# Both attentions of a fused two-layer kernel in new orders, the first one's sums of values in two halves

## The chip, the cores and the metric

One core of one Trainium2 chip. The metric is the device time of one execution in microseconds (us). TensorE is called PE, VectorE DVE, ScalarE ACT, GpSimd POOL and SyncE SP, as in the profile.

## What is computed

Two transformer layers over x of shape [8, 512, 128], all float32, each an attention and a feed-forward part with a layer norm behind each:

```
x = layernorm(x + attention0(x))      # 16 heads of 8, relative positions clipped to +-64
x = layernorm(x + ffn0(x))
x = layernorm(x + attention1(x))      # 16 heads of 8, sinusoidal relative shift
x = layernorm(x + ffn1(x))

# attention0, per batch and head (8 x 16 = 128 heads):
scores = Q K^T + take(Q pos_key^T, clip(k - q + 64)) + take(K pos_query^T, clip(q - k + 64))^T
probs  = softmax(scores * scale);  ctx = probs V
```

Attention1 differs in the form of its position scores; softmax and the sum of values are the same.

## The kernel before, in words

The program has five stages: an opening (projections, `opening`), the first attention (`attention(0)`, in the code `rel` is true), a mixing stage (feed-forward 0 and the projections of layer 1), the second attention (`attention(1)`) and a dense stage. An attention goes over 128 heads of 512 queries and 512 keys. One **step** works for one head `j`; the engines run it in parallel from five programs whose orders are written out by hand and joined by semaphores: `tensor_step`, `vector_step`, `scalar_step` and `sync_step`. Eight steps are unrolled in a loop; four of them (`GROUP`) make a group.

What a step does, with its four tiles k = 0 to 3 of 128 queries (`NT` = 4):

- `score_tile` (L821, L823, in the first attention also L827) makes a score tile in one of four PSUM banks, `score_ahead` tiles ahead (6 in the first attention, 7 in the second). It waits for the exp that empties its bank. In the first attention L827 writes a corner into the shared bank `other`, and so waits for the mask copy of the tile before.
- DVE: `mix` (L908, first attention only) copies that corner in by a mask; `finish` (L920) adds a band of position scores; `row_max` (L928) takes the maximum. `key_out` (L755, first) and `edge_out` (L933, second) copy a product of the position part out of PSUM, once in a step.
- ACT: `exp_tile` (L980), 4 or 5 tiles ahead; `copy_turned` (L987) copies a turned block out of PSUM; `corr_out` (L761, first attention); `group_out` (L993) copies the sums of a finished group, on the last step of each group, behind the second turned block.
- PE: `turn` (L842) transposes the 512 x 128 probabilities of key block k, four transposes of 128 x 128, into bank 5 or 6. `weigh` (L855) is the sum of values: for key block k of four heads of the group before, four matmuls of 32 columns by 512 queries (two instructions each), all adding to `cbank`. One such k is done in each step, so a group is summed during the four steps after it. `key_side` (L741) and `correction` (L748, L749) in the first attention, `edge` (L722) in the second, make the position part for a head some steps ahead. Bank 5 is shared with `key_side`, bank 6 with `correction`; in the second attention bank 4 takes `edge`.
- SP issues every DMA. In the first attention in each step: `shear_b_write` (L646), `shear_b_read` (L652), `head_load` (two halves, L608 and L609), `shear_a_read` (L640), `shear_a_write` (L634 for the next head); on a group's last step also `tab_load` (L621), three `offset_load` (L628, L629), the group's store (L671) and the next values (L673). `shear_b_write` waits for `corr_out`. The head loaded in one step is `key_side`'s in the next (`LOAD_AHEAD` 8, `KEY_AHEAD` 7).

The order of PE in a step before the change, and of ACT:

```
PE,  first:   score turn0 SUM | score turn1 key_side | score turn2 | score turn3 | correction
PE,  second:  score turn0 SUM | score turn1 edge     | score turn2 | score turn3
ACT, both:    exp copy0 | exp copy1 [group_out] | exp copy2 | exp copy3 | (first: corr_out)
DVE, first:   4 x (mix, row_max, finish), key_out behind the second
DVE, second:  4 x (finish, row_max), edge_out
```

The waits of `turn`: in the first attention turn0 for the last copy of the head before, turn1 for `corr_out`, turn2 for copy1, turn3 for `key_out`; in the second each turn for the copy two before.

Of the kernel before, what the change touches and what calls it, by code (L numbers as in the profile page):

```python
# [21 lines left out]
B, T, C = 8, 512, 128  # L22
H = 16
DH = C // H
NT = T // 128
NHEAD = B * H
# [31 lines left out]
VW = 32  # L58
BASE = 32
# [5 lines left out]
def build(nc, t):  # L65

    top = ExitStack()
    with top:
# [430 lines left out]
        def attention(layer):  # L499

            rel = layer == 0
# [287 lines left out]
            def program(block, before, after):  # L789
# [72 lines left out]
                def tensor_step(pe, i, j, left, weighed=True):  # L862
                    own = Head(i, j)
                    for k in range(NT):
                        if left >= (k + score_ahead) // NT:
                            score_tile(pe, *ahead(i, j, k, score_ahead))
                        turn(pe, own, k)
                        if k == 0 and weighed:
                            weigh(pe, Head(i, j - j % GROUP - GROUP), j % GROUP)
                        if not rel and k == 1 and left >= CORR_AHEAD:  # L870
                            pe.wait_ge(corr_copied, BASE + own.n + CORR_AHEAD)
                            edge(pe, Head(i, j + CORR_AHEAD), corr_bank)
                        if rel and k == 1 and left >= KEY_AHEAD:
                            pe.wait_ge(copied, BASE + 4 * own.n + 1)
                            key_side(pe, Head(i, j + KEY_AHEAD), key_bank)
                    if rel and left >= CORR_AHEAD:
                        pe.wait_ge(copied, BASE + 4 * own.n + 3)
                        correction(pe, Head(i, j + CORR_AHEAD))

                @block.tensor  # L880
                def _(pe):
# [16 lines left out]
                    for k in range(NT):  # L898
                        weigh(pe, Head(loops, FIRST + last - GROUP), k)
# [34 lines left out]

                @block.vector
                def _(v):
# [11 lines left out]
                    def vector_step(i, j, left):  # L948
                        for k in range(NT):

                            if left >= (k + score_ahead) // NT:
                                if rel:
                                    mix(v, *ahead(i, j, k, score_ahead))
                                else:
                                    finish(v, *ahead(i, j, k, score_ahead))
                            if left >= (k + score_ahead - 1) // NT:
                                row_max(v, *ahead(i, j, k, score_ahead - 1))
                            if rel and left >= (k + score_ahead) // NT:
                                finish(v, *ahead(i, j, k, score_ahead))
                            if not rel and k == 3 and left >= CORR_AHEAD:  # L960
                                edge_out(v, Head(i, j + CORR_AHEAD))
                            if rel and k == 1 and left >= KEY_AHEAD:
                                key_out(v, Head(i, j + KEY_AHEAD), key_bank)

                    for j in range(FIRST):
                        vector_step(0, j, NHEAD)
# [3 lines left out]
                    for j in range(last):  # L970
                        vector_step(loops, FIRST + j, last - 1 - j)
                        after.vector_tail(v, last - 1 - j)

# [22 lines left out]
                def _(act):  # L996
# [3 lines left out]
                    def scalar_step(i, j, left, weighed=True):  # L1000
                        own = Head(i, j)
                        for k in range(NT):
                            if left >= (k + exp_ahead) // NT:
                                exp_tile(act, *ahead(i, j, k, exp_ahead))
                            copy_turned(act, own, k)
                            if k == 1 and weighed and j % GROUP == GROUP - 1:
                                group_out(act, Head(i, j - j % GROUP - GROUP))
                        if rel and left >= CORR_AHEAD:
                            corr_out(act, Head(i, j + CORR_AHEAD))

# [8 lines left out]
                    group_out(act, Head(loops, FIRST + last - GROUP))  # L1019
# [1015 lines left out]
```

## Time and profile before

| | us |
|---|---|
| median of 3 runs | 1965.22 (1956.04 to 1966.07) |
| profiled execution | 1965.38 |
| its span on the core | 1963.2 |
| first attention, undisturbed part | 200 to 830 of the span |
| second attention, undisturbed part | 1065 to 1580 of the span |

Busy shares over the whole span: PE 88%, DVE 74%, ACT 75%, POOL 4%; DMA queues 67% of the 16 engines. The shares are means over five stages with different limits, so they are to be read by stretch. In a timeline row the columns are the start, the duration, the engine, the line of kernel.py, the operation, its tiles and shapes, the number of instructions merged into the row, and in brackets the idle time of that engine ahead of it and what ended it. PEld is the weight load of PE, SPq a DMA issue of SP.

### The profile page before, as it was taken

The numbers are of one execution on the slowest core, as the hardware profiler recorded it, in microseconds if no ns is written. First come the engines' busy times: TensorE is split into PE (matmuls) and PEld (weight loads), VectorE is DVE, ScalarE is ACT, GpSimd is POOL, SyncE is SP. The second block draws the span as 40 slices with busy tenths as digits, with TensorE's granted clock in tenths as the row PEclk, the third lists the DMA queues.
The fourth block names the chain that finished last, engine by engine and source line by source line (L and its number), as shares of the span: only waits on it lengthen the run. The fifth ranks groups of instructions, "written<-read, shape, count | busy, mean of one in ns | idle before, by whom it ended". The sixth has DMA issues, their size and how long they took to land.

```text
span 1963.2 us, 44049 instructions
## 1 busy us (share of the span) xinstructions
PE 1728.0 (88%) x11694; PEld 1040.9 (53%) x11694; DVE 1446.4 (74%) x3501; ACT 1475.8 (75%) x2605; POOL 80.2 (4%) x102
## 2 busy tenths in 40 slices
PE   5479999999999999977767999999999989999998
PEld 2145555555555555545444655655666544545454
DVE  5568888888888888876977888888888873244322
ACT  4458888888888888876878999999999974232221
POOL 0000000000000000003520000000000000000000
PEclk8679999999999999998978999999999989999999
DMA  6788888888888888865999777777777771001000
GB/s 207 281 249 256 268 265 261 263 263 266 264 266 265 264 259 264 259 183 158 342 338 297 217 213 210 213 212 214 210 214 213 209 211 44 21 27 37 21 6 11
DMA packets 414359, 404.44 MB, mean 206 GB/s; under 512 B 36969, under 2 KB 334561, under 8 KB 414177
## 3 DMA queue, kind: packets, MB, share of 16 engines
q1 hardware_dynamic: 414305, 403.80, 67.3%
q8 instruction: 24, 0.39, 0.1%
q14 instruction: 30, 0.25, 0.0%
HBM read 226.89 MB, written 176.30 MB: 205 GB/s over the span
## 4 chain that ended last, share of the span: by engine, by line
PE 48%; issue 13%; ACT 11%; DVE 9%; SPq 8%; DMA 6%; POOL 0%; DVEq 0%; ACTq 0%; POOLq 0%
PE bank L842 12%; PE bank L1847 11%; PE bank L855 9%; ACT a_probt L987 5%; PE bank L821 4%; DVE a_negmax L928 3%; DMA a_stks<-stack 3%; ACT a_prob L980 3%; DVE a_keyside L755 2%; DVE bank L908 2%; PE bank L823 2%; PE bank L1839 1%; PE bank L1840 1%; PE bank L1868 1%; PE bank L722 1%
## 5 line engine op out<-in xcount | busy, mean ns | idle before, releaser
L980 ACT ACTIVATE a_prob<-bank,a_negmax 128x512 f32<-128x512 f32 x1024 | 738.2, 721 | 44.7 <-DVE a_negmax L928 43.2
L928 DVE TENSOR_REDUCE a_negmax<-bank 128x1 f32<-128x512 f32 x1024 | 698.3, 682 | 0.2 <-issue 0.2
L842 PE MATMUL bank<-ident,a_prob 128*128 128x128 f32 x4096 | 646.5, 281 | 56.8 <-ACT a_probt L987 49.0
L987 ACT COPY a_probt<-bank 128x512 f32<-128x512 f32 x1024 | 619.5, 605 | 97.4 <-PE bank L842 85.6
L842 PEld LDWEIGHTS bank<-ident,a_prob 128*128 128x128 f32 x4096 | 451.5, 142 | 174.9 <-issue 70.7
L920 DVE TENSOR_TENSOR bank<-bank,a_band 128x128 f32<-128x128 f32 (+3 forms) x1024 | 349.5, 341 | 81.6 <-PE bank L823 66.5
L821 PE MATMUL bank<-a_stks 74*128 74x192 bf16 (+7 forms) x1024 | 324.9, 317 | 31.5 <-ACT a_prob L980 29.4
L855 PE MATMUL bank<-a_probt,a_vs 128*32 128x512 f32 x2048 | 275.3, 612 | 12.8 <-ACT a_probt L987 12.8
L821 PEld LDWEIGHTS bank<-a_stks 74*128 74x128 bf16 (+1 forms) x1024 | 100.2, 98 | 260.0 <-ACT a_prob L980 215.0
L908 DVE COPY_PREDICATED bank<-a_mask,bank 128x128 f32<-128x128 uint32 (+1 forms) x512 | 139.4, 272 | 112.0 <-PE bank L827 109.7
L823 PE MATMUL bank<-a_stks 74*128 74x320 bf16 (+5 forms) x768 | 201.8, 263 | 0.0
L1913 DVE TENSOR_TENSOR d_drop<-bank,d_s 128x128 f32<-128x128 f32 x32 | 7.1, 283 | 170.4 <-PE bank L1868 170.4
L748 PE MATMUL bank<-ident,a_sheared 128*128 128x128 f32 x512 | 106.5, 285 | 19.4 <-DMA a_sheared<-shear_a 15.0
L827 PE MATMUL bank<-a_stks 74*128 74x128 bf16 (+1 forms) x512 | 110.4, 216 | 10.9 <-DVE bank L908 2.7
L1847 PE MATMUL bank<-d_ha,d_h1T 128*128 128x512 f32 x256 | 112.3, 592 | 0.0
L1847 PE MATMUL bank<-d_hb,d_h2T 128*128 128x512 f32 x256 | 111.2, 592 | 0.0
L755 DVE COPY a_keyside<-bank 128x512 f32<-128x512 f32 x128 | 87.2, 681 | 24.8 <-PE bank L741 24.4
L749 PE MATMUL bank<-a_tabs,a_stks 65*128 65x128 bf16 x512 | 97.5, 225 | 0.0
L761 ACT COPY a_corr<-bank 128x512 f32<-128x512 f32 x128 | 76.4, 597 | 23.2 <-DMA shear_b<-a_corr 11.9
L748 PEld LDWEIGHTS bank<-ident,a_sheared 128*128 128x128 f32 x512 | 74.3, 145 | 34.7 <-issue 21.5
L1898 ACT ACTIVATE d_hb<-bank,d_fs 128x512 f32<-128x512 f32 x32 | 22.0, 687 | 90.6 <-PE bank L1847 90.6
L1903 ACT ACTIVATE d_hc<-bank,d_fs 128x512 f32<-128x512 f32 x32 | 22.0, 687 | 87.6 <-PE bank L1847 87.6
(178 smaller groups left out, 1622.7 us busy)
## 6 DMA issues: line engine op xcount, KB each, us to landing
a_band<-shear_b SPq DMA_DIRECT2D x128, 512.0 KB, 4.9
shear_a<-a_keyside SPq DMA_DIRECT2D x128, 256.0 KB, 3.7
a_sheared<-shear_a SPq DMA_DIRECT2D x128, 256.0 KB, 3.7
shear_b<-a_corr SPq DMA_DIRECT2D x128, 256.0 KB, 2.8
shear_e<-a_corr SPq DMA_DIRECT2D x128, 256.0 KB, 2.2
a_band<-shear_e SPq DMA_DIRECT2D x128, 256.0 KB, 3.1
a_stks<-stack SPq DMA_DIRECT2D x256, 96.0 KB, 3.0
a_stks<-stack SPq DMA_DIRECT2D x384, 48.0 KB, 2.5
```

The source lines that it names most:

```text
L748: pe.matmul(corr_bank[:, q], sheared[h.slot % 4][:, q], ident[:, :], is_transpose=True, start=True, stop=False)
L755: v.tensor_copy(keyside[h.slot % 4][:, :], source[:, :]).then_inc(key_copied, 1)
L821: last = pe.matmul(score[:, 0:c], k[:, qlo, q], k[:, keys, 0:c], start=True, stop=True)
L823: last = pe.matmul(score[:, c:T], k[:, qhi, q], k[:, keys, c:T], start=True, stop=True)
L842: last = pe.transpose(turned_bank[k][:, n * 128:(n + 1) * 128], prob[h.slot % 2][:, n, k * 128:(k + 1) * 128], ident[:, :])
L855: pe.matmul(cbank[32 * j:32 * j + VW, :], vs[g][:, at:at + VW], probt[h.slot + j][:, k, :], start=(k == 0), stop=(k == NT - 1)).then_inc(p ...
L908: v.copy_predicated(score[:, a:e], mask[:, 0:e - a], other[:, 0:e - a]).then_inc(fixed, 1)
L920: v.tensor_tensor(score[:, a:e], score[:, a:e], band[h.slot % bands][:, n, w:w + e - a], ALU.add).then_inc(added, 1)
L928: v.tensor_reduce(negmax[h.slot % 2][:, n:n + 1], score[:, :], AX.X, ALU.max, negate=True).then_inc(maxed, 1)
L980: nc.scalar.activation(prob[h.slot % 2][:, n, :], score[:, :], ACT.Exp, bias=negmax[h.slot % 2][:, n:n + 1]).then_inc(exped, 1)
L987: nc.scalar.copy(probt[h.slot][:, k, :], turned_bank[k][:, :]).then_inc(copied, 1)
L1847: last = pe.matmul(dst[:, :], w[:, k, 128 * m:128 * m + 128], src[:, k, :], start=(k == 0), stop=(k == KH - 1))
```

## The change

The four step functions are split into one for each attention, written out without the loop over k. In the first attention `weigh` takes a range of columns: in the steps of a group's second to fourth head it does queries 0 to 255 behind turn1 and queries 256 to 511 behind turn2; in the step of the group's first head it does all 512 behind turn1. In the second attention turn0 and turn1 stand together, then a score tile, then the sum of all 512; turn2 and turn3 stand together; `edge` moves to the end of the step. ACT's order becomes exp, copy, copy, exp, exp, copy, (group copy in the first), and so on. The group copy of the second attention moves from ACT to DVE, behind the second maximum of the last step of a group. SP's program is not touched.

```
PE,  first:   score turn0 score turn1 SUM(a) key_side score turn2 SUM(b) score turn3 correction
PE,  second:  score turn0 turn1 score SUM score turn2 turn3 score edge
ACT, first:   exp copy0 copy1 exp exp copy2 [group_out] exp copy3 corr_out
ACT, second:  exp copy0 copy1 exp exp copy2 copy3 exp
DVE, second:  finish max finish max [group copy] finish max finish max edge_out
```

```diff
-                def weigh(pe, h, k):
+                def weigh(pe, h, k, cols):
...
-                        pe.matmul(cbank[32 * j:32 * j + VW, :], vs[g][:, at:at + VW], probt[h.slot + j][:, k, :],
-                                  start=(k == 0), stop=(k == NT - 1)).then_inc(pv_mm, 1)
+                        part = pe.matmul(cbank[32 * j:32 * j + VW, cols], vs[g][:, at:at + VW], probt[h.slot + j][:, k, cols],
+                                         start=(k == 0), stop=(k == NT - 1 and cols.stop == T))
+                        if cols.stop == T:
+                            part.then_inc(pv_mm, 1)
...
+                def shifted_tensor_step(pe, i, j, left, weighed=True):
                     own = Head(i, j)
...
+                    score_ahead_of(pe, i, j, left, 0)
+                    turn(pe, own, 0)
+                    score_ahead_of(pe, i, j, left, 1)
+                    turn(pe, own, 1)
+                    if weighed:
+                        weigh(pe, Head(i, j - j % GROUP - GROUP), j % GROUP, slice(0, T // 2 if j % GROUP else T))
+                    if left >= KEY_AHEAD:
+                        pe.wait_ge(copied, BASE + 4 * own.n + 1)
+                        key_side(pe, Head(i, j + KEY_AHEAD), key_bank)
+                    score_ahead_of(pe, i, j, left, 2)
+                    turn(pe, own, 2)
+                    if weighed and j % GROUP:
+                        weigh(pe, Head(i, j - j % GROUP - GROUP), j % GROUP, slice(T // 2, T))
+                    score_ahead_of(pe, i, j, left, 3)
+                    turn(pe, own, 3)
+                    if left >= CORR_AHEAD:
                         pe.wait_ge(copied, BASE + 4 * own.n + 3)
                         correction(pe, Head(i, j + CORR_AHEAD))
+
+                def edged_tensor_step(pe, i, j, left, weighed=True):
+                    own = Head(i, j)
+                    score_ahead_of(pe, i, j, left, 0)
+                    turn(pe, own, 0)
+                    turn(pe, own, 1)
+                    score_ahead_of(pe, i, j, left, 1)
+                    if weighed:
+                        weigh(pe, Head(i, j - j % GROUP - GROUP), j % GROUP, slice(0, T))
+                    score_ahead_of(pe, i, j, left, 2)
+                    turn(pe, own, 2)
+                    turn(pe, own, 3)
+                    score_ahead_of(pe, i, j, left, 3)
+                    if left >= CORR_AHEAD:
+                        pe.wait_ge(corr_copied, BASE + own.n + CORR_AHEAD)
+                        edge(pe, Head(i, j + CORR_AHEAD), corr_bank)
...
+                def edge_group_out(v, h):
+
+                    v.wait_ge(pv_mm, BASE + 16 * (h.use(GROUP) + 1))
+                    v.wait_ge(out_written, BASE + 16 * h.use(GROUP))
+                    v.tensor_copy(outs[:, :], cbank[:, :]).then_inc(out_copied, 1)
...
+                    def edged_vector_step(i, j, left, weighed=True):
+                        finish_ahead_of(i, j, left, 0)
+                        max_ahead_of(i, j, left, 0)
+                        finish_ahead_of(i, j, left, 1)
+                        max_ahead_of(i, j, left, 1)
+                        if weighed and j % GROUP == GROUP - 1:
+                            edge_group_out(v, Head(i, j - j % GROUP - GROUP))
+                        finish_ahead_of(i, j, left, 2)
...
+                    def shifted_scalar_step(i, j, left, weighed=True):
                         own = Head(i, j)
...
+                        exp_ahead_of(i, j, left, 0)
+                        copy_turned(act, own, 0)
+                        copy_turned(act, own, 1)
+                        exp_ahead_of(i, j, left, 1)
+                        exp_ahead_of(i, j, left, 2)
+                        copy_turned(act, own, 2)
+                        if weighed and j % GROUP == GROUP - 1:
+                            group_out(act, Head(i, j - j % GROUP - GROUP))
+                        exp_ahead_of(i, j, left, 3)
+                        copy_turned(act, own, 3)
+                        if left >= CORR_AHEAD:
                             corr_out(act, Head(i, j + CORR_AHEAD))
```

`score_ahead_of`, `exp_ahead_of`, `finish_ahead_of`, `max_ahead_of` and `mix_ahead_of` hold the condition and the call that stood in the loops.

## Rows read from the trace of the kernel before

**Rows 1.** Busy time by stretch: engines in us, PE's clock, DMA share, GB/s.

```profile
400.00:500.00 100.00, 92.68 (x733) 57.16 (x732) 84.31 (x218) 86.51 (x156) 0.00 (x0) 1.00 0.85 262
...
1200.00:1300.00 100.00, 93.77 (x780) 59.85 (x778) 87.82 (x201) 98.14 (x185) 0.00 (x0) 1.00 0.72 212
```

**Rows 2.** Groups of instructions, from 200 to 800 and from 1100 to 1500 us.

```profile
L755 DVE COPY a_keyside<-bank 128x512 f32<-128x512 f32 x100 | 68.1, 681 | 4.2 <-PE bank L741 4.2
...
L933 DVE COPY a_corr<-bank 128x512 f32<-128x512 f32 x89 | 60.4, 679 | 0.0
```

**Rows 3.** Waits from 200 to 800 us: total, times, longest.

```profile
PEld bank L842 <- ACT a_probt L987: 37.0, 87, 0.4
PEld bank L827 <- DVE bank L908: 36.5, 101, 0.4
```

**Rows 4.** Timeline from 400 to 426 us, SP's issues and the key product.

```profile
400.64 0.37 SPq L646 DMA_DIRECT2D shear_b<-a_corr  x1
...
409.55 0.35 SPq L609 DMA_DIRECT2D a_stks<-stack  x1
...
415.48 0.39 PE L741 MATMUL bank<-a_stks,a_tabs 65*128 65x512 bf16 x1 [0.94 <-DMA a_stks<-stack]
...
419.30 0.37 SPq L646 DMA_DIRECT2D shear_b<-a_corr  x1
...
425.24 0.37 SPq L646 DMA_DIRECT2D shear_b<-a_corr  x1
```

**Rows 5.** Timeline of the second attention: three sums of values in a row.

```profile
1202.40 1.06 PE L855 MATMUL bank<-a_probt,a_vs 128*32 128x512 f32 x8
...
1207.57 1.07 PE L855 MATMUL bank<-a_probt,a_vs 128*32 128x512 f32 x8 [0.41 <-ACT a_probt L987]
...
1211.73 1.07 PE L855 MATMUL bank<-a_probt,a_vs 128*32 128x512 f32 x8
```

**Rows 6.** Timeline of ACT: exps seven pairs apart, and a group copy.

```profile
1046.52 0.74 ACT L980 ACTIVATE a_prob<-bank,a_negmax 128x512 f32<-128x512 f32 x1
...
1053.85 0.87 ACT L980 ACTIVATE a_prob<-bank,a_negmax 128x512 f32<-128x512 f32 x1
...
1204.75 0.63 ACT L993 COPY a_outs<-bank 128x512 f32<-128x512 f32 x1
```

**Rows 7.** Timeline of ACT: activations behind activations.

```profile
1020.41 0.69 ACT L1413 ACTIVATE m_qv<-bank,m_uvs 128x512 f32<-128x512 f32 x1
1020.99 0.69 ACT L1414 ACTIVATE m_full<-bank,m_uvs 128x512 f32<-128x512 f32 x1
...
1035.32 1.48 ACT L980 ACTIVATE a_prob<-bank,a_negmax 128x512 f32<-128x512 f32 x2 [1.71 <-DVE a_negmax L928]
```

**Rows 8.** Timeline of the second attention: DVE, and a score tile with its add.

```profile
1201.26 0.29 DVE L920 TENSOR_TENSOR bank<-bank,a_band 128x128 f32<-128x128 f32 x1
...
1201.46 0.68 DVE L928 TENSOR_REDUCE a_negmax<-bank 128x1 f32<-128x512 f32 x1
...
1202.06 0.68 DVE L933 COPY a_corr<-bank 128x512 f32<-128x512 f32 x1
...
1202.65 0.29 DVE L920 TENSOR_TENSOR bank<-bank,a_band 128x127 f32<-128x127 f32 x1
...
1214.29 0.33 PE L821 MATMUL bank<-a_stks 96*128 96x385 bf16 x1
...
1214.85 0.29 DVE L920 TENSOR_TENSOR bank<-bank,a_band 128x128 f32<-128x128 f32 x1
```

**Rows 9.** Timeline of the first attention: PE around the sums of values.

```profile
406.15 0.63 PE L842 MATMUL bank<-ident,a_prob 128*128 128x128 f32 x4
...
406.71 1.06 PE L855 MATMUL bank<-a_probt,a_vs 128*32 128x512 f32 x8
...
407.96 0.63 PE L842 MATMUL bank<-ident,a_prob 128*128 128x128 f32 x4
...
408.43 0.38 PE L741 MATMUL bank<-a_stks,a_tabs 65*128 65x512 bf16 x1
```

**Rows 10.** The head load's second half (L609), 200 to 800 us: issue to landing.

```profile
DMA to landing us min/median/max: 3.0/4.0/6.1
```

More of the change, by code:

```diff
@@ L858, in ahead, with score_ahead_of @@
                 def ahead(i, j, k, tiles):
                     return Head(i, j + (k + tiles) // NT), (k + tiles) % NT
-                def tensor_step(pe, i, j, left, weighed=True):
+                def score_ahead_of(pe, i, j, left, k):
+                    if left >= (k + score_ahead) // NT:
+                        score_tile(pe, *ahead(i, j, k, score_ahead))
+                def shifted_tensor_step(pe, i, j, left, weighed=True):
                     own = Head(i, j)
[L864 to L876, printed above, removed]
@@ L880, in _ @@
+                tensor_step = shifted_tensor_step if rel else edged_tensor_step
                 @block.tensor
@@ L898, in _ @@
                     for k in range(NT):
-                        weigh(pe, Head(loops, FIRST + last - GROUP), k)
+                        weigh(pe, Head(loops, FIRST + last - GROUP), k, slice(0, T))
                 def mix(v, h, n):
@@ L946, in _, with mix_ahead_of @@
                             row_max(v, *ahead(0, 0, 0, n - 1))
[L948 to L963, printed above, removed]
+                    def mix_ahead_of(i, j, left, k):
+                        if left >= (k + score_ahead) // NT:
+                            mix(v, *ahead(i, j, k, score_ahead))
@@ L965, in _ @@
+                    vector_step = shifted_vector_step if rel else edged_vector_step
                     for j in range(FIRST):
-                        vector_step(0, j, NHEAD)
+                        vector_step(0, j, NHEAD, weighed=False)
                     with v.Fori(0, loops) as i:
@@ L972, in _ @@
                         after.vector_tail(v, last - 1 - j)
+                    if not rel:
+                        edge_group_out(v, Head(loops, FIRST + last - GROUP))
                 def exp_tile(act, h, n):
@@ L998, in _, with exp_ahead_of, edged_scalar_step @@
                         exp_tile(act, *ahead(0, 0, 0, n))
-                    def scalar_step(i, j, left, weighed=True):
+                    def exp_ahead_of(i, j, left, k):
+                        if left >= (k + exp_ahead) // NT:
+                            exp_tile(act, *ahead(i, j, k, exp_ahead))
+                    def shifted_scalar_step(i, j, left, weighed=True):
                         own = Head(i, j)
[L1002 to L1008, printed above, removed]
-                            corr_out(act, Head(i, j + CORR_AHEAD))
+                        exp_ahead_of(i, j, left, 0)
[8 more added lines that the diff above has]
+                        copy_turned(act, own, 3)
+                        if left >= CORR_AHEAD:
+                            corr_out(act, Head(i, j + CORR_AHEAD))
+                    def edged_scalar_step(i, j, left, weighed=True):
+                        own = Head(i, j)
+                        exp_ahead_of(i, j, left, 0)
+                        copy_turned(act, own, 0)
+                        copy_turned(act, own, 1)
+                        exp_ahead_of(i, j, left, 1)
+                        exp_ahead_of(i, j, left, 2)
+                        copy_turned(act, own, 2)
+                        copy_turned(act, own, 3)
+                        exp_ahead_of(i, j, left, 3)
+                    scalar_step = shifted_scalar_step if rel else edged_scalar_step
                     for j in range(FIRST):
@@ L1018, in _ @@
                         after.scalar_tail(act, last - 1 - j)
-                    group_out(act, Head(loops, FIRST + last - GROUP))
+                    if rel:
+                        group_out(act, Head(loops, FIRST + last - GROUP))
             def of_first(move):
```

25 lines of the change are left out of this document (added).

## The prediction

> **What bounds the kernel now.** I read the busy time by stretches first. In the first attention PE is busy 93% of its time and DMA 85%; in the second, ACT is busy 98% and PE 94% [rows 1]. The reader should see two stages with different limits, so each is costed alone. A step is one head of 128; counting one instruction that comes once in a step gives 600 us / 100 = 6.00 us for a step of the first attention and 400 / 89 = 4.49 us for one of the second [rows 2].
>
> First attention. PE's busy share hides waits of its loading side: in 100 steps 37.0 us for ACT's copies of turned blocks and 36.5 us for DVE's mask copy, 0.73 us in a step [rows 3]. An undisturbed step takes 5.94 us (425.24 less 419.30, two issues of shear_b one step apart), so PE's own work is about 5.21 us. A second chain runs through SP, and it decides every second group of four heads [rows 4]: the issue of shear_b at 400.64; eight more issues and the head load's second half at 409.55, 8.91 us later; the load lands and key_side's matmul, which stood waiting 0.94 us, starts at 415.48, 5.93 us later; the next shear_b at 419.30, 3.82 us; one free step of 5.94. The sum is 24.60 us, against 4 x 5.94 = 23.76 for a group that nothing holds.
>
> Second attention. PE comes to its sums of values at 1202.40, 1207.57 and 1211.73 [rows 5]: a step with the copy of a finished group (L993, on ACT) lasts 5.17 us, one without 4.16. The 0.41 us before 1207.57 is PE waiting for ACT's last copy, because the group's first sum stands right behind the first turn. ACT has no slack: in seven exp-and-copy pairs without a wait, starts go from 1046.52 to 1053.85 while the exp's recorded length grows from 0.74 to 0.87 us [rows 6]. End to end that is 7.46 / 7 = 1.066 us for a pair, 4.27 for a step; the outs copy (0.63 us) is on top.
>
> **The change, part by part. Second attention.** The group copy leaves ACT for DVE. Four steps cost ACT 4 x 4.27 = 17.08 us against 4 x 4.49 = 17.96 now. It also moves the sums behind the second turn and the next score tile, so ACT's last copy is over by then: the 0.41 us goes. Exps and copies go in pairs of a kind; an activation behind an activation starts 0.58 us after it [rows 7], as a copy behind an exp does, so I cost that at nothing. DVE takes the copy. Its add, maximum and corner copy step by 0.20, 0.60 and 0.60 us [rows 8], so a step is 4 x 0.80 + 0.60 = 3.80, and with a quarter of a group copy 3.95: under 4.27. What is late next is a loop over two steps. Exp 0.75 and signal 0.05; two score tiles 0.48 (PE's free 4.16 less four turns at 0.47, the sums at 1.12 and the edge product at an estimated 0.22, over four tiles); sums 1.12; two turns 0.94; a tile to its band add 0.56 [rows 8]; add, maximum, corner copy, add, maximum, add 2.40; maximum and signal 0.72; then exp and two copies 1.55. That is 8.57 us, or 4.29 for a step. I take 4.30 (ends: 4.27 and 4.49). The edge product moves to the end of the step; the corner copy behind it on DVE comes after a maximum of 0.60 us, which covers the product's 0.22; uncovered it would cost those 0.22 us a step. SP's order is unchanged. Gain 4 x 0.19 = 0.76 us for a group, 29 groups between the two mixed stretches: 22 us.
>
> **First attention, on PE.** Three heads of a group sum in two halves. A whole set of eight matmuls occupies PE about 1.00 us: from its start to the next turn is 1.25 with one score tile, at 0.25, between them; the turn ahead takes 0.56 where a turn before a key product takes 0.47 [rows 9], so going into the sums costs 0.1 more. A half lies between 0.50 (everything halves) and 1.00 (nothing does); I take 0.56, since columns halve and the start does not. With 0.12 to go in, a pair costs 1.36 against 1.12: +0.24. For it the waits go. The score tile that used to wait for the mask copy now has half a sum ahead of it, and ACT's two copies in a row are done before their banks are wanted. So a step costs 5.21 + 0.24 = 5.45 where it is split, and about 5.3 in the first head of each group, which is not split. On PE alone a group takes 21.7 us.
>
> The Trainium skill has a rule against the split (TensorEngine Tiling (Array Packing), Key Properties): changing the tiling mode drains the engine. The sums use 32-column tiles between full-width products, so the halves double those changes. The trace agrees in kind, with the 0.1 us ahead of the sums; without the rule the pair would cost 1.12 and a step 5.21.
>
> **First attention, through SP.** The 8.91 us of issues stay, in the same order. The landing stays or grows. From the late key product to the next shear_b issue: ACT's chain gave 3.82; PE's is now 0.22 + 0.3 + 0.47 + 0.68 + 0.3 + 0.47, the correction to its copy 0.94, the copy 0.60 and 0.1, in all 4.1. The free step falls to 5.45. In a held group the wait from load to key product is on average 48.00 - 23.76 - 8.91 - 3.82 - 5.94 = 5.57 us; so it becomes 8.91 + 5.57 + 4.1 + 5.45 = 24.0 against 24.24. In the other group the chain lies just under 23.76 now; with the median landing of 4.0 [rows 10] it would be 22.6 after the change, with the most that today's 23.76 allows 23.5, and I take 23.2, because this load follows a bunch of transfers. Two groups: 47.2 against 48.0. DMA is busy 85% and the free steps bring transfers 0.49 us closer, so I add 0.2 us of landing to each: 47.6. Fourteen such pairs: 6 us, where PE alone would promise (48.0 - 43.4) x 14 = 64. The group copy, now behind the third copy on ACT, is still over before SP reaches its store at the end of its series; the exp behind it is late by 0.3 us, which the turn it feeds can bear.
>
> **The sum.** The profiled execution took 1965.38 us (span 1963.2), the same as the median of 1965.22. 1965.4 - 22 - 6 = 1937. Opening, mixing and dense stages stay.
>
> **Rivals.** (1) The loads land early: if the landing shrank towards its minimum of 3.0 [rows 10], the chain would be about 22 us and PE's 21.7 would rule. That is 54 us from the first attention: 1889. For it: nothing in SP's order forbids it. Against: DMA at 85% now would be at 93% or more. Chance 0.10. (2) The second attention keeps part of its wait, the two-step loop being longer than I can read: at 4.40 its gain is 10 us: 1949. Chance 0.14. (3) Slower: the backlog of transfers. Its place is the head load issued behind the group's store, values and band reads. If the free steps only pile transfers up, that landing decides: a gain of 28 us is gone when the landings of two groups grow by 2.0 us together, and at 4 us it is 28 us slower, 1993. For it: landings reach 6.1 already [rows 10], and the load is on the chain. Against: the mean rate hardly changes when the group hardly gets shorter. Chance 0.07. (4) Halves cost as much as wholes, 1.12 each: +0.44 behind the key product and +0.88 in the free step, 1.32 x 28 = 37 us: 1974. Chance 0.08. (5) An exp behind an exp costs more: two in a row stand 0.79 us apart [rows 7], 1.48 less 0.69. At 0.79 ACT's step would be 4.27 + 0.42 = 4.69, 23 us slower there: 1982. Against it, the maxima that released those exps came every 0.80 us. Chance 0.05. (6) The edits cancel and nothing moves: 1965, chance 0.04. My forecast has 0.52; its own range is 1926 to 1948.
>
> **How the numbers follow.** About 0.5% is what a measurement can tell here, 1955.6 to 1975.2. Faster: 0.52 + 0.10 + 0.14 = 0.76. Same: (4) and (6), 0.12. Slower: (3) and (5), 0.12. The range runs from 1900, on the way to rival 1 and holding a third of its chance, to 1975, above (2), (6) and (4): outside are (3), (5) and the rest of (1), 0.19.
>
> **What would show it.** Right: steps of the second attention all near 4.3 us, L993's successor on DVE, no 0.41 us wait for ACT; in the first attention the PE waits for DVE's mask copy mostly gone, and in their place one wait per group of 1 to 2 us at key_side for the head load, in both groups of a loop. Wrong: score or turn waits still spread over the first attention's steps; half sums above 0.7 us each; steps of 4.4 us or more in the second; a granted clock under 1.00 behind the longer waits.

## The result, and the profile after

| | before | after |
|---|---|---|
| median | 1962.15 us (13 runs) | 1941.74 us (13 runs) |
| ratio, 95% interval | | 0.9899 (0.9886 to 0.9913) |
| profiled execution, span | 1965.38, 1963.2 us | 1944.98, 1943.2 us |
| last key product of the first attention, start | 839.80 us | 829.28 us |
| step of the first attention (96 steps) | 5.99 us | 5.90 us |
| step of the second attention (96 steps) | 4.493 us | 4.374 us |

The change made the kernel 1.0% faster, 20 us, where 28 were forecast. A step is read here more exactly than by counting: from the start of the 21st key product (first attention) or corner copy (second) to that of the 117th, over 96. The timeline of the changed kernel, these four instructions:

```profile
199.16 0.38 PE L741 MATMUL bank<-a_stks,a_tabs 65*128 65x512 bf16 x1 [1.60 <-issue]
...
765.56 0.38 PE L741 MATMUL bank<-a_stks,a_tabs 65*128 65x512 bf16 x1 [1.18 <-issue]
...
1131.62 0.68 DVE L961 COPY a_corr<-bank 128x512 f32<-128x512 f32 x1
...
1551.54 0.68 DVE L961 COPY a_corr<-bank 128x512 f32<-128x512 f32 x1
```

566.40 / 96 = 5.90 and 419.92 / 96 = 4.374. The same instructions of the kernel before stand 574.98 and 431.29 us apart. The busy time by stretch, changed kernel, in the columns of [rows 1]:

```profile
400.00:500.00 100.00, 93.71 (x872) 62.85 (x870) 88.54 (x229) 89.24 (x162) 0.00 (x0) 0.98 0.89 273
...
1200.00:1300.00 100.00, 98.41 (x814) 60.94 (x811) 93.76 (x214) 99.65 (x187) 0.00 (x0) 1.00 0.78 223
```

ACT is now nearly full in the second attention, as meant: 99.65 of 100 us in this stretch, 395.14 of 400 from 1100 to 1500 us. In the first there is something new: the granted clock is 0.98, where it was 1.00. The waits of the changed kernel from 200 to 800 us (total, times, longest), against [rows 3]:

```profile
PEld bank L741 <- issue: 53.0, 34, 2.8
...
PE bank L741 <- DMA a_stks<-stack: 23.7, 13, 2.3
...
PEld bank L827 <- DVE bank L936: 16.4, 61, 0.5
...
PEld bank L842 <- ACT a_probt L1053: 2.5, 12, 0.2
```

The two old waits fell from 36.5 and 37.0 us to 16.4 and 2.5. What took their place is the key product L741, which now waits for the head load. The chain forecast from [rows 4] can be read again from the timeline, PE and SP:

```profile
350.37 0.37 SPq L646 DMA_DIRECT2D shear_b<-a_corr  x1
...
359.23 0.35 SPq L609 DMA_DIRECT2D a_stks<-stack  x1
...
364.85 0.39 PE L741 MATMUL bank<-a_stks,a_tabs 65*128 65x512 bf16 x1 [2.12 <-DMA a_stks<-stack]
...
370.25 0.37 SPq L646 DMA_DIRECT2D shear_b<-a_corr  x1
...
375.50 0.37 SPq L646 DMA_DIRECT2D shear_b<-a_corr  x1
```

The steps are 8.86 us of issues (forecast 8.91), 5.62 to the late key product (5.57), 5.40 to the next shear_b (forecast 4.1) and 5.25 for the free step (5.45): 25.1 us in all against 24.0. The 1.3 us too many in the third have their cause in the next rows, the same kernel by stretches of 2 us:

```profile
364.00:366.00 2.00, 1.15 (x12) 0.83 (x16) 0.60 (x1) 0.00 (x0) 0.00 (x0) 1.00 1.10 398
366.00:368.00 2.00, 2.00 (x16) 1.34 (x17) 1.70 (x6) 1.27 (x2) 0.00 (x0) 0.57 0.69 214
368.00:370.00 2.00, 2.00 (x15) 1.53 (x14) 0.69 (x2) 1.02 (x2) 0.00 (x0) 0.58 0.54 203
370.00:372.00 2.00, 2.00 (x21) 1.07 (x20) 1.94 (x6) 2.00 (x5) 0.00 (x0) 1.00 0.62 155
```

PE stood idle 2.12 us and came back to work; a little more than a microsecond later its clock was near the lower level of 1.2 GHz for about 4 us. The step from this key product to the next takes 6.74 us; a step of the same place in a group whose clock stayed takes 5.22. Between 200 and 800 us PE's timeline has 13 waits at the key product of more than 1.4 us; behind 11 of them the next step takes 6.7 to 6.8 us, and behind none of the shorter waits. That is 11 x 1.5 = 16 us, in all but one case in the group of each pair that was held before. The length of the wait alone does not decide it: two waits of 1.72 and 1.75 us were not followed by a fall, and in e11 below, whose first attention has the same code, only 7 of 13 were, a wait of 2.28 us not among them. Executions of the same kernel differ too, and the longer ones show the lower clock: the quickest of the changed kernel's 13 took 1933.19 us at a mean granted clock of 0.955, the slowest 1954.47 us at 0.946.

The half sums, in the timeline of PE:

```profile
371.02 0.64 PE L855 MATMUL bank<-a_probt,a_vs 128*32 128x256 f32 x8
371.59 0.39 PE L741 MATMUL bank<-a_stks,a_tabs 65*128 65x512 bf16 x1
...
372.63 0.64 PE L855 MATMUL bank<-a_probt,a_vs 128*32 128x256 f32 x8
373.20 0.31 PE L821 MATMUL bank<-a_stks 74*128 74x320 bf16 x1
```

A half occupies PE 0.57 us where 0.56 was taken. In the second attention, 1100 to 1500 us, there is a wait that the kernel before did not have:

```profile
DVE bank L948 <- DMA a_band<-shear_e: 12.3, 31, 1.1
```

### The profile page after: what moved, and what is told of

The parts are those of the page before. It is cut to its first block, busy times and chain, and to the rows that moved or that the text cites. A ratio compares the mean times of both kernels' runs of the same rounds, so it can differ in the third digit from the quotient of the medians.

```text
span 1943.2 us, 45550 instructions
## 1 busy us (share of the span) xinstructions
PE 1721.4 (89%) x12438; PEld 1057.7 (54%) x12438; DVE 1463.4 (75%) x3533; ACT 1453.5 (75%) x2573; POOL 80.1 (4%) x102
## 4 chain that ended last, share of the span: by engine, by line
PE 43%; SPq 16%; issue 13%; DMA 12%; DVE 8%; ACT 7%; DVEq 0%; POOL 0%; ACTq 0%; POOLq 0%
PE bank L1936 11%; PE bank L842 10%; PE bank L855 6%; DMA a_band<-shear_e 6%; DMA a_stks<-stack 4%; PE bank L821 4%; DVE a_negmax L956 3%; ACT a_probt L1053 3%; ACT a_prob L1046 2%; PE bank L823 2%; PE bank L1928 1%; PE bank L1929 1%; DVE bank L948 1%; PE bank L741 1%; PE bank L748 1%
## 5 line engine op out<-in xcount | busy, mean ns | idle before, releaser
L1046 ACT ACTIVATE a_prob<-bank,a_negmax 128x512 f32<-128x512 f32 x1024 | 696.4, 731 | 54.7 <-DVE a_negmax L956 52.6
L1053 ACT COPY a_probt<-bank 128x512 f32<-128x512 f32 x1024 | 584.9, 624 | 71.7 <-PE bank L842 70.8
L842 PE MATMUL bank<-ident,a_prob 128*128 128x128 f32 x4096 | 603.8, 281 | 21.8 <-ACT a_probt L1053 15.5
L855 PE MATMUL bank<-a_probt,a_vs 128*32 128x256 f32 (+1 forms) x2792 | 298.1, 501 | 0.4 <-ACT a_probt L1053 0.4
L761 ACT COPY a_corr<-bank 128x512 f32<-128x512 f32 x128 | 76.1, 595 | 39.1 <-PE bank L749 25.1
L741 PE MATMUL bank<-a_stks,a_tabs 65*128 65x512 bf16 x128 | 51.3, 400 | 58.1 <-DMA a_stks<-stack 25.9
L749 PE MATMUL bank<-a_tabs,a_stks 65*128 65x128 bf16 x512 | 101.4, 230 | 0.0
L855 PEld LDWEIGHTS bank<-a_probt,a_vs 128*32 128x32 f32 x2792 | 56.3, 109 | 68.2 <-issue 68.0
```

The costliest lines, as they stand in the source:

```text
L842: last = pe.transpose(turned_bank[k][:, n * 128:(n + 1) * 128], prob[h.slot % 2][:, n, k * 128:(k + 1) * 128], ident[:, :])
L855: part = pe.matmul(cbank[32 * j:32 * j + VW, cols], vs[g][:, at:at + VW], probt[h.slot + j][:, k, cols], start=(k == 0), stop=(k == NT - 1 ...
L1046: nc.scalar.activation(prob[h.slot % 2][:, n, :], score[:, :], ACT.Exp, bias=negmax[h.slot % 2][:, n:n + 1]).then_inc(exped, 1)
L1053: nc.scalar.copy(probt[h.slot][:, k, :], turned_bank[k][:, :]).then_inc(copied, 1)
```

## The experiments

Each ratio is to the kernel before on the same chip. The steps are those of one profiled execution each. The first attention's differs between executions once PE waits there for loads: 5.86 to 5.95 us in the six runs that have the changed kernel's code for that stage, 5.91 to 5.95 in the four of them that ran on one chip (e1, e5, e6, e7). So for the second attention the step from the trace decides, not the total.

| run | median us | ratio, 95% interval | step 1st | step 2nd |
|---|---|---|---|---|
| changed kernel | 1941.74 | 0.9899 (0.9886 to 0.9913) | 5.90 | 4.374 |
| e1 first only | 1959.53 | 0.9986 (0.9965 to 1.0006) | 5.91 | 4.493 |
| e2 second only | 1947.65 | 0.9928 (0.9903 to 0.9953) | 5.97 | 4.366 |
| e3 sums whole | 1939.84 | 0.9889 (0.9859 to 0.9919) | 5.79 | 4.383 |
| e4 head load first | 1898.50 | 0.9662 (0.9628 to 0.9695) | 5.51 | 4.383 |
| e5 group copy on ACT | 1953.39 | 0.9939 (0.9917 to 0.9960) | 5.93 | 4.380 |
| e6 edge product mid-step | 1953.55 | 0.9926 (0.9897 to 0.9955) | 5.95 | 4.385 |
| e7 band read first | 1965.50 | 1.0001 (0.9970 to 1.0033) | 5.93 | 4.483 |
| e8 e4 and e7 | 1906.82 | 0.9708 (0.9680 to 0.9736) | 5.40 | 4.485 |
| e9 e3 and e4 | 1908.99 | 0.9722 (0.9706 to 0.9738) | 5.61 | 4.385 |
| e10 old order, head load first | 1957.31 | 0.9965 (0.9949 to 0.9980) | 5.94 | 4.487 |
| e11 early edge copy | 1926.98 | 0.9822 (0.9806 to 0.9839) | 5.86 | 4.275 |
| e12 e4 and e11 | 1876.00 | 0.9563 (0.9547 to 0.9579) | 5.46 | 4.280 |

**e1 and e2: one attention at a time.** In e1 the second attention's PE and ACT run the old order again, group copy on ACT (the first added line of each pair); in e2 the first one's (the second). The old step functions that both add are those of the kernel before and are not shown.

```diff
-                tensor_step = shifted_tensor_step if rel else edged_tensor_step
+                tensor_step = shifted_tensor_step if rel else old_tensor_step
+                tensor_step = old_tensor_step if rel else edged_tensor_step
...
-                    scalar_step = shifted_scalar_step if rel else edged_scalar_step
+                    scalar_step = shifted_scalar_step if rel else old_scalar_step
+                    scalar_step = old_scalar_step if rel else edged_scalar_step
```

> Only the first attention in the new order; the second as before, its group copy on ACT. If the two stages add up as the two traces say (last key product 10.5 us earlier, 2 to 4 us of it lost in the mixing stage), this is 7 to 10 us under before: ratio 0.995 to 0.9965. Rival: the first attention's gain is all given back behind it and the whole 20 us is the second's: ratio 0.999 to 1.001.

> Only the second attention in the new order, with its group copy on DVE. Sum theory: 12 to 14 us under before, ratio 0.993 to 0.994. Rival (all of the gain is the second's): ratio 0.990. Steps of three in four at 4.26 us, and band waits of DVE on shear_e as in the changed kernel, in both.

e2 came out as the sum theory has it, 0.9928: 14 us, with an interval (9 to 19 us) that just leaves out the rival's 0.990. e1 shows 0.9986, 3 us, with an interval that holds both no change and 7 us; it lies between what the two theories forecast and tells them apart no better than that. In its profiled execution the last key product starts at 830.32 us, 9.5 us earlier than before, and the first corner copy of the second attention 7.0 us earlier (10.5 and 8.2 in the changed kernel), so part of the gain is lost in the mixing stage. By the medians about two thirds of the gain are the second attention's.

**e3: the sums whole.**

```diff
-                        weigh(pe, Head(i, j - j % GROUP - GROUP), j % GROUP, slice(0, T // 2 if j % GROUP else T))
+                        weigh(pe, Head(i, j - j % GROUP - GROUP), j % GROUP, slice(0, T))
...
-                    if weighed and j % GROUP:
-                        weigh(pe, Head(i, j - j % GROUP - GROUP), j % GROUP, slice(T // 2, T))
```

> The changed kernel, but every sum of values of the first attention whole, behind the second turn. If the head load's chain rules, the split gives nothing: the key product comes 0.4 us later in a step that waits for it anyway, and the work behind it is 0.5 us shorter. Then 0 to 10 us faster than the changed kernel (ratio to before 0.985 to 0.990), with shorter waits at key_side. Rival: the half behind the third turn is what covers the wait for the mask copy; without it PE waits 0.35 us a step again for DVE and the kernel is 5 to 10 us slower than the changed one (0.992 to 0.995).

The ratio of 0.9889 is not apart from the changed kernel's. The trace shows two changes that go against each other: the waits of PE's loads for the mask copy are back, and the wait at the key product is shorter. From 200 to 800 us, e3:

```profile
PEld bank L741 <- issue: 41.1, 29, 2.3
...
PEld bank L827 <- DVE bank L934: 38.2, 104, 0.5
...
PE bank L741 <- DMA a_stks<-stack: 12.4, 12, 1.4
```

Both parts happened: the mask wait of 38.2 / 104 = 0.37 us a step that the rival named, and the shorter waits of the first theory. Its longest wait at the key product is 1.4 us where the changed kernel had 2.3, and its granted clock from 200 to 800 us is 1.00. In the medians the two sides cancel. The profiled execution, the quickest of its four, does better: its step is 5.79 us against 5.90. With the load as the bound, splitting the sums buys nothing here, and whole sums may be a little quicker; that is not shown.

**e4: the head load first.** SP issues the load ahead of shear_b's write and read.

```diff
+                    if left >= LOAD_AHEAD:
+                        hold(sp, maxed, 4 * (n + 1))
+                        head_load(sp, Head(i, j + LOAD_AHEAD))
                     if left >= CORR_AHEAD - 1:
                         hold(sp, added, 4 * (n + 1))
                         shear_b_write(sp, Head(i, j + CORR_AHEAD - 1))
...
-                    if left >= LOAD_AHEAD:
-                        hold(sp, maxed, 4 * (n + 1))
-                        head_load(sp, Head(i, j + LOAD_AHEAD))
```

> The changed kernel, with SP issuing the head load ahead of shear_b's write and read in each step, 1.9 us earlier. If the late head load is what holds the groups, PE's waits at key_side from 200 to 800 us fall from 34 us to under 8, the granted clock of the first attention returns to 1.00, a pair of groups goes from 47.4 us towards 44.5, and the kernel is 30 to 40 us faster than the changed one (ratio 0.970 to 0.975). Rival: DMA throughput is the bound (share 0.87 to 0.90 now); then another landing is late instead (the band or the sheared block), and the gain stays under 12 us (ratio over 0.984).

0.9662, a step of 5.51 us: 43 us under the changed kernel, a little more than the 30 to 40 expected; the last key product starts 43.6 us earlier. The rival falls: DMA's share rose to 0.91 and no other landing took the load's place as the bound, though most other transfers land later (the sheared block's median went from 3.7 to 4.2 us). The busy time of e4 from 200 to 800 us:

```profile
200.00:800.00 600.00, 575.39 (x5432) 380.38 (x5430) 550.63 (x1418) 551.47 (x1007) 0.10 (x1) 1.00 0.91 283
```

and its waits there:

```profile
PEld bank L741 <- issue: 15.4, 25, 0.8
...
PE bank L748 <- DMA a_sheared<-shear_a: 10.9, 18, 1.2
```

The wait of PE at L741 for the load is gone from the list, the clock is 1.00, and PE is busy 96% of the stretch. The late head load was the bound of the changed first attention. Of the 43 us some 16 are the clock, which no longer falls. Next in line is the sheared block, 0.1 us a step.

The edit does more than move two issues 1.9 us forward. In the changed kernel the load stood behind shear_b's write, and that write waits for ACT's correction copy, which comes at the end of the chain that begins with the key product. SP's own waits from 200 to 800 us, in the changed kernel and in e4:

```profile
SPq L598 <- ACT a_corr L761: 103.7, 65, 3.4
...
SPq L598 <- ACT a_corr L761: 1.3, 4, 0.4
```

So in e4 SP hardly ever waits for that copy, and a late key product no longer makes the next load late in this way. No run separates the two things that the edit does, the earlier place and the wait that no longer stands ahead of the load.

**e10 and e9: what SP's order was worth in the old order, and what the split is worth in the new one.** e10 is the kernel before with e4's edit; e9 has both e3's and e4's.

> The kernel before, with the head load first and nothing else. There PE's step of 5.94 us is the bound and the load costs only 0.05 us a step: 4 to 8 us faster than before (ratio 0.996 to 0.998). Rival: SP's order was as much a limit of the old order; then a step falls well under 5.94 and the ratio under 0.99.

> The kernel with the head load first, but the first attention's sums whole. With the load out of the way PE rules, and now the split should show its worth: whole, PE waits again 0.35 us a step for the mask copy and some for copied blocks, against 0.24 us that the halves cost. A step of 5.6 to 5.7 us against 5.51, so 10 to 20 us slower than with the halves (ratio to before 0.971 to 0.976). Rival: the halves cost as much as they hide also here: within 5 us (0.964 to 0.969).

Both as the first theory has them. e10's step is 5.94 us, the free step of [rows 4], and the gain 0.35%: in the old order the step on PE, its own waits included, was the bound. They are still there (200 to 800 us, e10):

```profile
PEld bank L842 <- ACT a_probt L987: 43.8, 101, 0.4
PEld bank L827 <- DVE bank L908: 35.5, 101, 0.4
```

e9 takes 5.61 us a step, e4 5.51: with the load out of the way the halves are worth 0.1 us a step, 10 us in the medians. The two ran on different chips, but their intervals against the kernel before lie apart, and the other two executions with halves and the load first took 5.40 and 5.46 us a step. So the edits bring more together than one by one: the load's edit alone gives 0.35%, the new orders alone 1.0%, together 3.4%.

**e5: the group copy back on ACT,** behind the third turned copy, in the new order.

```diff
                         copy_turned(act, own, 2)
+                        if weighed and j % GROUP == GROUP - 1:
+                            group_out(act, Head(i, j - j % GROUP - GROUP))
                         copy_turned(act, own, 3)
...
-                        if weighed and j % GROUP == GROUP - 1:
-                            edge_group_out(v, Head(i, j - j % GROUP - GROUP))
```

The copy of the very last group, behind the loop, goes back to ACT too (not shown).

> The changed kernel, but the second attention's group copy stays on ACT, behind the third turned copy of a group's last step. If ACT is the bound there (98 to 99.7% busy), a group takes 0.48 us more of it: from 17.5 us to 17.6 to 18.0, part of it hidden by the band wait, so 3 to 12 us slower than the changed kernel (ratio to before 0.9915 to 0.996). Rival: the order of turns and sums alone brought the gain and the band wait is the bound: no difference (0.989 to 0.991).

The total (0.9939) fell inside the first theory's range, but the trace gives another reason for a part of it: in its profiled execution the first attention, whose code is unchanged, ran at 5.93 us a step. The second attention's step is 4.380 against 4.374. So the rival is right about the stage, and both theories are right about a bound. The two rows of e5, busy time and waits from 1100 to 1500 us:

```profile
1100.00:1500.00 400.00, 392.76 (x3202) 240.31 (x3201) 364.42 (x823) 400.00 (x756) 0.00 (x0) 1.00 0.76 218
```

```profile
DVE bank L948 <- DMA a_band<-shear_e: 0.8, 4, 0.2
```

ACT is busy all 400.00 us and the band wait is 0.8 us: (4 x 4.27 + 0.48) / 4 = 4.39. Without the copy ACT could run at 4.27, but then the bands come late and give 4.37. One bound was exchanged for another of the same length. The moved copy, by itself, brought nothing; the new orders of PE and ACT, which were not tested apart, brought the gain from 4.493 to 4.380.

**e6: the edge product in the middle of the step,** behind the sums, its copy on DVE left at the end.

```diff
+                    if left >= CORR_AHEAD:
+                        pe.wait_ge(corr_copied, BASE + own.n + CORR_AHEAD)
+                        edge(pe, Head(i, j + CORR_AHEAD), corr_bank)
                     score_ahead_of(pe, i, j, left, 2)
...
-                    if left >= CORR_AHEAD:
-                        pe.wait_ge(corr_copied, BASE + own.n + CORR_AHEAD)
-                        edge(pe, Head(i, j + CORR_AHEAD), corr_bank)
```

> The changed kernel, with the second attention's edge product back in the middle of the step, behind the sums. DVE copies its result after four maxima either way, so nothing should come of it: within 3 us of the changed kernel (0.988 to 0.992). Rival: the product's late place makes corr, its write to shear_e and so the bands late; then the band waits (12.3 us from 1100 to 1500) shrink and it is 5 to 12 us faster (0.984 to 0.987).

4.385 us a step: no effect, as the first theory has it; the total, 0.9926, is a hair above its range and its first attention took 5.95 us a step. DVE's copy decides when the transfer starts, not the product.

**e7 and e8: the band read ahead of the write.**

```diff
-                    if left >= CORR_AHEAD:
-                        edge_write(sp, Head(i, j + CORR_AHEAD))
                     if weighed and left >= CORR_AHEAD - 1 or 0 < j < FIRST and not weighed:
                         if weighed:
                             hold(sp, added, 4 * (n + CORR_AHEAD - bands))
                         edge_read(sp, Head(i, j + CORR_AHEAD - 1))
+                    if left >= CORR_AHEAD:
+                        edge_write(sp, Head(i, j + CORR_AHEAD))
```

> The changed kernel, with SP issuing the band's read ahead of the edge's write in each step of the second attention: 0.6 us earlier, and no longer behind DVE's corner copy. If the late band is what keeps the group above four times 4.27 us, DVE's waits on shear_e fall under 3 us from 1100 to 1500, the step goes from 4.374 to 4.27 to 4.31 us, and the kernel is 6 to 12 us faster than the changed one (0.984 to 0.987). Rival: DVE's own two-step loop is as long, and the wait only covers it: 0 to 3 us (0.988 to 0.990).

> Head load ahead of shear_b's write in the first attention and band read ahead of the edge's write in the second. If both theories hold, the two gains add: 0.966 less 0.004 to 0.006, ratio 0.960 to 0.963, about 1885 to 1891 us. If the band theory falls, 0.965 to 0.967.

Neither theory: the step rose from 4.374 to 4.483 us, and in e8, whose ratio of 0.9708 is above both forecasts, it rose by as much over e4 (4.485 against 4.383). The waits of e7, 1100 to 1500 us:

```profile
DVE bank L948 <- DMA a_band<-shear_e: 25.0, 44, 1.3
```

and its transfers there (the last number is the median us from issue to landing; 3.3 and 2.3 in the changed kernel):

```profile
a_band<-shear_e SPq DMA_DIRECT2D x90, 256.0 KB, 3.3
shear_e<-a_corr SPq DMA_DIRECT2D x89, 256.0 KB, 3.6
```

The write now follows a read of the same size and lands 1.3 us later, and the next step's read has to wait for that landing. SP's own waits in e7 show it:

```profile
SPq L598 <- DMA shear_e<-a_corr: 39.0, 65, 1.4
```

So the edit did not bring the bands earlier; it made them later. It speaks for late bands as the bound (more of the wait, a longer step), but it was no test of an early band. e11 is.

**e11: the edge copy two maxima earlier.** The product goes ahead of the sums, its copy behind the second maximum. No transfer changes its place; SP's whole step starts earlier.

```diff
                     score_ahead_of(pe, i, j, left, 1)
+                    if left >= CORR_AHEAD:
+                        pe.wait_ge(corr_copied, BASE + own.n + CORR_AHEAD)
+                        edge(pe, Head(i, j + CORR_AHEAD), corr_bank)
                     if weighed:
...
-                    if left >= CORR_AHEAD:
-                        pe.wait_ge(corr_copied, BASE + own.n + CORR_AHEAD)
-                        edge(pe, Head(i, j + CORR_AHEAD), corr_bank)
...
                         max_ahead_of(i, j, left, 1)
+                        if left >= CORR_AHEAD:
+                            edge_out(v, Head(i, j + CORR_AHEAD))
                         if weighed and j % GROUP == GROUP - 1:
...
-                        if left >= CORR_AHEAD:
-                            edge_out(v, Head(i, j + CORR_AHEAD))
```

> The changed kernel, with the second attention's edge product ahead of the sums and its copy on DVE behind the second maximum instead of the fourth, so that SP's whole step there, band read included, can start about 2.5 us earlier; no transfer changes its place. If late bands hold the group, the waits on shear_e fall from 12.3 us to under 3 between 1100 and 1500 and the step from 4.374 to 4.28 to 4.32 us, 6 to 11 us. Rival: DVE's two-step loop or ACT holds it there anyway: 4.35 us or more. The step read from the trace decides, since the first attention's time differs between chips by some us.

> Head load first and the early edge copy together. If the band theory holds, the second attention's step is 4.28 to 4.32 us here as well, and the kernel is 6 to 11 us faster than with the head load first alone: ratio to before 0.960 to 0.964, about 1887 us. Rival: 0.965 to 0.970.

The band wait is gone from e11's list, the step is 4.275 us, and ACT is busy all the time:

```profile
1100.00:1500.00 400.00, 398.14 (x3278) 249.96 (x3271) 382.19 (x867) 400.00 (x750) 0.00 (x0) 1.00 0.79 224
```

That is ACT's own rate of 4.27 from [rows 6] to a hundredth. With the bands early the step falls by 0.10 us, 12 us of the stage, and stops at ACT: the late band was the bound of the changed second attention, and the rival falls. e11's ratio is 0.9822 against 0.9899, 15 us; the 3 us more are within what the first attention differs by (5.86 us a step here).

**e12** has both mended stages: 1876.0 us, 0.9563, 66 us (3.4%) under the changed kernel. That is some 7 us better than the forecast of 0.960 to 0.964; the second attention's step is as forecast, 4.280, and the first one's is 5.46 us against e4's 5.51. The band wait from 1100 to 1500 us is a single one of 1.2 us there.

## Why the prediction was right, and where it was off

The time was forecast at 1937 us and came out at 1941.7, inside the likeliest case's own range of 1926 to 1948; against the kernel before on the same chip the gain was 20 us instead of 28. Both stages gained, and ACT's pace and the chain through SP are mechanisms that the forecast named. But the next bound of the second attention was another one, and it was in part luck that the sum of the first came out right.

- **Second attention, ACT's pace.** Right. Full ACT gives 4.27 us a step; e11 reaches 4.275. An exp behind an exp cost no more than behind a copy (rival 5 falls), since e11 has two such pairs in every step and ACT's pace there is the 4.27 of before.
- **Second attention, the next bound.** Wrong in its place. The forecast named DVE's two-step loop at 4.29 and took 4.30, with all steps near 4.3 as its sign; in the changed kernel they go from 3.88 to 5.34 us between 1100 and 1300 us. The loop is no longer than ACT's pace. One step of the changed kernel in which no band is late takes 4.26 us, but a loop over two steps needs more of them in a row; e5 has three, between its copies of groups, with the corner copy still at the end of the step (12.77 us, 4.26 each). In the changed kernel:

```profile
1235.69 0.68 DVE L961 COPY a_corr<-bank 128x512 f32<-128x512 f32 x1
1239.95 0.68 DVE L961 COPY a_corr<-bank 128x512 f32<-128x512 f32 x1
```

and in e5:

```profile
1172.32 0.68 DVE L961 COPY a_corr<-bank 128x512 f32<-128x512 f32 x1
...
1185.09 0.68 DVE L961 COPY a_corr<-bank 128x512 f32<-128x512 f32 x1
```
What held 4.374 was a transfer, passed over with the sentence "SP's order is unchanged". Its order was, but its margin was not: each step got shorter while the landing (median 3.1 us before, 3.3 after) and SP's series did not, and the band read is issued about one step ahead of its use. The term "gain 4 x 0.19 = 0.76 us for a group" measured 4 x 0.119 = 0.48; over 29 groups 14 us instead of 22, which e2 shows as 14.
- **The group copy.** The forecast gave it part of the gain. e5 shows that it has none of it in this kernel. Once bands are early it should count: e11 reaches 4.275, while e5, with the copy on ACT and ACT busy all the time, takes 4.380. No run has e11's early edge copy together with the group copy on ACT.
- **First attention, PE.** Right in kind. The two waits fell as forecast, a half was 0.57 us against 0.56. A free split step takes 5.2 us, not 5.45: PE's own work in the old step, 5.21 us, had been put too high. The two rows counted do not hold all of PE's waits; the same list of the kernel before has, for example,

```profile
PE bank L842 <- ACT a_probt L987: 28.3, 158, 0.2
```

which is 0.28 us a step and 4.8 us in all after the change. That it is this wait that makes up the difference is likely, not shown. e4 and e9 show the halves worth 0.1 us when the load no longer holds.
- **First attention, the head load.** The mechanism was right, and e4 shows it: the chain through SP took back what PE would have gained. Of 64 us that PE's order alone promised, the forecast left 6; the last key product started 10.5 us earlier, and e4 found 43 of the rest with one edit on SP. Terms: issues and landing right within 0.05 us; the key product to the next shear_b 5.40 instead of 4.1, because the clock fell; the free step 5.25 instead of 5.45; the held group 24.5 us on average instead of 24.0, the other group of a pair, as a rule without a fall of the clock, 22.7 us instead of 23.2. The errors cancelled, which was luck: 8 steps took 47.2 us, as forecast before the 0.4 for backlog.
- **The clock.** The prediction named a lower clock behind longer waits as a sign that would make it wrong, and gave it no price. It was there, at 1.5 us each, 16 us between 200 and 800 us; the total held only because the free steps were shorter than forecast.
- **The rule of the Trainium skill** (TensorEngine Tiling (Array Packing), Key Properties: a change of the tiling mode drains the engine). The turn ahead of a first half takes 0.57 us where one ahead of a key product took 0.47, so it pays its way in; ahead of a second half it takes 0.53. The trace agrees in kind, but no row here shows a drain as such. e9 against e4 shows that what the halves cover is worth more.

What stays open: how much of the first attention's gain survives the mixing stage, where e1 and the changed kernel lose about 2.4 us each in their profiled executions; what decides whether a wait of 1.4 us or more is followed by a fall of the clock; and why the first attention still differs by 0.11 us a step (5.40, 5.46 and 5.51 us in e8, e12 and e4) where the load is first and the clock stays.

## What to carry to other kernels

When a step is made shorter by better order on the engines, look first at every transfer with a fixed number of steps of lead: its lead in microseconds shrinks with the step, although nobody has touched its queue. Here the load that came late, one in four, stood behind a long series in the same queue (a group's tables, offsets, store and values) and behind a wait for ACT's correction copy, which comes late itself when a load was late; no run shortened the series alone. Put the load that is needed soonest at the head of the step, ahead of any issue that waits for the engines. And a copy taken off a full engine brought nothing here while the next bound, a late band, stood as close: test the move alone before counting it.

## What was not expected of the hardware

- One wait of 2.1 us of PE, in a stage in which it is busy 92% of its time, was followed by about 4 us at a granted clock of 0.57 and 0.58, and cost 1.5 us more than the wait itself. Of 13 waits over 1.4 us 11 were followed so in the changed kernel, and 7 of 13 in e11. The waits of up to 1.4 us in e3 and of up to 1.2 us in the kernel before left it at 1.00.
- A write of 256 KB issued about 0.6 us behind a read of 256 KB landed in 3.6 us where it took 2.3 ahead of it, while the read stayed at 3.3 (medians, e7): exchanging the two helped neither.
- With DMA at a share of 0.91 and 283 GB/s (e4) the head load's second half still landed sooner, 3.3 us in the median against 4.4 in the changed kernel at 0.88, while the transfers behind it landed later (the tables 5.4 us against 3.4). For this load its place in the queue mattered more than the mean rate.
